# Radial products on halves of the array's rows, with the bias added by bf16 products of ones

## The reference

```python
R = relu(abs_distances[:, None] @ w1 + b1) @ w2 + b2      # (E, 384), HIDDEN = 64
Y = spherical_harmonics(rel_vec)
Fj = features[src]
...
acc = acc + _NORM[i] * jnp.einsum('euv,ef,evi,ofi->euo', Rb[..., k], Yf, Fb, C)
...
out = out.at[dst].add(msg)
x = _layernorm(x + out)
```

## Time and profile before

| | |
|---|---|
| time, median of 3 runs | 1985.52 us (1982.97 to 1986.45) |
| span of the profiled execution | 1707.1 us |
| median less span | 278.4 us |
| busy in the span: PE, DVE, POOL, ACT | 1315.9, 1193.5, 1068.9, 858.9 us |
| mean granted TensorE clock | 0.846 of full speed |
| layer 1 | 1139 to 1556 us |

### The profile page before, as it was taken

How to read it: one execution, slowest core, us unless ns; L and a number is a source line. 1 busy time by engine, 2 the same in 40 slices (tenths; PEclk the granted TensorE clock), 3 DMA queues, 4 the chain that set the end, 5 groups by cost and what they waited for, 6 DMA issues and landing times.

```text
span 1707.1 us, 25367 instructions
## 1 busy us (share of the span) xinstructions
PE 1315.9 (77%) x6200; PEld 957.6 (56%) x6200; DVE 1193.5 (70%) x3648; ACT 858.9 (50%) x2256; POOL 1068.9 (63%) x1168
## 2 busy tenths in 40 slices
PE   5699993686513777665778999958999999996673
PEld 1388881242212555554655666635777777775563
DVE  9699995677512443676667999964777777774776
ACT  0167770011101222666775777735666666664884
POOL 7777778777777777774111444448877887830444
PEclk8599996577555999888888999977999999997655
DMA  1000000123224988665555666531222222213785
GB/s 41 13 14 13 14 14 20 47 72 79 67 68 127 257 250 246 171 174 145 132 138 140 179 184 189 163 95 32 58 58 57 58 64 67 59 42 78 196 216 157
DMA packets 298498, 178.98 MB, mean 105 GB/s; under 512 B 28715, under 2 KB 290032, under 8 KB 298352
## 3 DMA queue, kind: packets, MB, share of 16 engines
q1 hardware_dynamic: 219712, 116.54, 26.0%
q0 software_dynamic: 29008, 36.18, 8.3%
q10 hardware_dynamic: 49632, 24.65, 5.0%
HBM read 111.18 MB, written 66.07 MB: 104 GB/s over the span
## 4 chain that ended last, share of the span: by engine, by line
PE 42%; POOL 28%; issue 16%; DVE 8%; DMA 2%; DVEq 2%; SPq 1%; ACT 1%; POOLq 0%; ACTq 0%
PE bank L1025 12%; POOL gat L511 12%; POOL lined L518 11%; PE bank L994 7%; PE bank L1018 7%; DVE res L1308 5%; PE bank L945 3%; POOL out L591 3%; PE bank L947 3%; PE bank L1034 3%; PE bank L1003 3%; PE bank L987 3%; DMA placed<-pay,pos_i 1%; DVEq L1308 1%; DVEq L1302 1%
## 5 line engine op out<-in xcount | busy, mean ns | idle before, releaser
L566 POOL DMA_INDIRECT gat<-x_d,src_i x196 | 253.2, 1292 | 59.0 <-issue 53.1
L511 POOL DMA_INDIRECT gat<-in_x,key_i x196 | 211.1, 1077 | 64.8 <-issue 62.4
L1308 DVE TENSOR_TENSOR res<-res,bank 128x128 f32 x588 | 168.4, 286 | 108.5 <-issue 24.4
L528 POOL DMA_INDIRECT placed<-pay,pos_i x196 | 191.9, 979 | 68.1 <-issue 65.6
L518 POOL DMA_INDIRECT lined<-in_x,other_i x196 | 195.8, 999 | 59.7 <-issue 59.7
L1025 PE MATMUL bank<-prod,ident 128*128 128x280 f32 x896 | 217.0, 400 | 0.0
L1025 PEld LDWEIGHTS bank<-prod,ident 128*128 128x128 f32 x896 | 171.0, 191 | 46.5 <-issue 0.6
L956 PE MATMUL bank<-woh,pw 128*128 128x128 f32 x784 | 135.4, 335 | 69.3 <-DVE woh L1287 33.4
L956 PEld LDWEIGHTS bank<-woh,pw 128*128 128x128 f32 x784 | 120.3, 238 | 85.5 <-DVE woh L1287 44.5
L56 ACT ACTIVATE xt<-bank 128x128 f32<-128x128 f32 x98 | 26.6, 271 | 269.6 <-PE bank L897 261.2
L1018 PE MATMUL bank<-rw,ht 65*128 65x384 f32 x392 | 141.3, 514 | 23.3 <-ACT ht L738 13.8
(11 more groups left out here) (204 smaller groups left out, 2840.5 us busy)
## 6 DMA issues: line engine op xcount, KB each, us to landing
pw<-placed SPq DMA_DIRECT2D x588, 68.0 KB, 2.1
pw<-placed SPq DMA_DIRECT2D x98, 272.0 KB
xin<-in_x_t SPq DMA_DIRECT2D x53, 256.0 KB, 3.2
placed<-pay SPq DMA_DIRECT2D x49, 272.0 KB, 2.4
x_d<-res POOLq DMA_DIRECT2D x49, 256.0 KB, 3.8
placed<-pay SPq DMA_DIRECT2D x28, 448.0 KB, 3.2
out<-out ACTq DMA_DIRECT2D x49, 256.0 KB, 2.7
xin<-in_x_t ACTq DMA_DIRECT2D x45, 256.0 KB, 3.6
```

The source lines that it names most:

```text
L511: pool.indirect_dma_start(gat[:, t, :], None, x, bass.IndirectOffsetOnAxis(ap=key_i[:, 0, t:t + 1], axis=0)).then_inc(s_gat, 16)
L528: pool.indirect_dma_start(placed[1].rearrange("t p r -> (t p) r"), bass.IndirectOffsetOnAxis(ap=pos_i[:, 1, t:t + 1], axis=0), pay[i % 4][ ...
L566: pool.indirect_dma_start(gat1[g % 3][:, k, :], None, x1_d, bass.IndirectOffsetOnAxis(ap=src_i[:, t:t + 1], axis=0)).then_inc(c_gat[g % 3] ...
L1308: add.up(dve.tensor_tensor(into, into, quarter(bank + k // G, k % G), ALU.add))
```

## The change

The products of R are split by the array's rows. `arow` and `ht` get 128 partitions: the tiles of a group with even numbers (0, 2, 4, 6) stand in partitions 0 to 63, those with odd numbers (1, 3, 5) in partitions 64 to 127, each 128 edges wide, so `ht[h]` is 128 partitions by 512 columns. `rw`, `rwc_sb` and their raw forms are held twice, once in each half. The row of ones is gone, so an f32 product has 64 rows. The bias is added by a bf16 product of its own in front of it, into the same bank: `unit`, ones of 64 rows by 128 columns, is held, and `rb3`, 64 rows by 384, is streamed, whose rows 0, 1 and 2 are the bias in three bf16 pieces that add up to it, the others zero. PE goes through a group in three pairs and a single tile: both waits for the banks and both products of ones stand in front of the two f32 products.

SP issues two DMAs for `arow` instead of one, and reads every second row of `ew_d` in each. The weights' DMAs move behind a wait for `s_rec` (line 1183's signal), in front of the first store of the placed rows, because `rw_raw` now shares memory with earlier arrays; there are 4 of them instead of 1, and one more for `rwc_sb`. DVE's `radial_weights` places and scales the bias too and splits it. A memset of `arow`'s spare corner takes the place of the memset of ones.

```diff
@@ load_weights, SP
-                sp.dma_start(arow[h][:, :].rearrange("p (t q) -> p t q", t=U),
-                             ew_d[U * g:U * g + U, :].partition_broadcast(HID)).then_inc(c_arow[h], 16)
+                for o in range(2):
+                    n = (U + 1 - o) // 2
+                    sp.dma_start(arow[h][HID * o:HID * o + HID, 0:P * n].rearrange("p (t q) -> p t q", t=n),
+                                 ew_d[U * g + o:U * g + U:2, :].partition_broadcast(HID)).then_inc(c_arow[h], 16)
@@ in front of SP's stores of the placed rows
+            sp.wait_ge(s_rec, 1)
+            for h in range(2):
+                sp.dma_start(rw_raw[HID * h:HID * h + HID, :], rwb[0:HID, :]).then_inc(s_rwld, 16)
+                sp.dma_start(rb_raw[HID * h:HID * h + HID, :], rwb[HID:HID + 1, :].partition_broadcast(HID)).then_inc(s_rwld, 16)
@@ hidden_3, ACT
-                act.wait_ge(c_arow[h], 16 * (g // 2 + 1))
+                act.wait_ge(c_arow[h], 32 * (g // 2 + 1))
-                act.activation(ht[h][0:HID, :], arow[h][:, :], ACT.Relu, bias=rwc_sb[:, 1:2], scale=rwc_sb[:, 0:1]).then_inc(c_ht, 1)
+                act.activation(ht[h][:, :], arow[h][:, :], ACT.Relu, bias=rwc_sb[:, 1:2], scale=rwc_sb[:, 0:1]).then_inc(c_ht, 1)
@@ radial, PE
-                for k in range(U):
-                    n = U * g + k
-                    wait(pe, c_rsb, n - 2)
-                    pe.matmul(psum[n % 3][:, 0:RC], ht[g % 2][:, P * k:P * k + P], rw[:, :, :].rearrange("p a b -> p (a b)"),
-                              start=True, stop=True).then_inc(c_r, 1)
+                for k in range(0, U, 2):
+                    pair = [(U * g + k + o, HID * o) for o in range(min(2, U - k))]
+                    for n, r in pair:
+                        wait(pe, c_rsb, n - 2)
+                        pe.matmul(psum[n % 3][:, 0:RC], unit[r:r + HID, :], rb3[r:r + HID, :, :].rearrange("p a b -> p (a b)"),
+                                  start=True, stop=False)
+                    for n, r in pair:
+                        pe.matmul(psum[n % 3][:, 0:RC], ht[g % 2][r:r + HID, P * (k // 2):P * (k // 2) + P],
+                                  rw[r:r + HID, :, :].rearrange("p a b -> p (a b)"), start=False, stop=True).then_inc(c_r, 1)
@@ radial_weights, DVE (combine(to, raw) is the 7 instructions of before)
+                dve.memset(unit[:, :], 1.0)
+                chain.up(combine(rw, rw_raw))
+                done(chain)
+                chain.up(combine(rb, rb_raw))
+                chain.up(dve.tensor_scalar(half[:, :], pcol[:, :], float(HID), -float(HID), ALU.is_ge, ALU.mult))
+                done(chain)
+                chain.up(dve.tensor_tensor(half[:, :], half[:, :], pcol[:, :], ALU.add))
+                done(chain)
+                for n in range(3):
+                    chain.up(dve.tensor_scalar(piece[:, n:n + 1], half[:, :], float(n), None, ALU.is_equal))
+                for n in range(3):
+                    chain.up(dve.tensor_copy(rb_h[:, :, :], rb[:, :, :]))
+                    done(chain)
+                    if n == 0:
+                        ins = dve.tensor_scalar(rb3[:, :, :], rb_h[:, :, :], piece[:, 0:1], None, ALU.mult)
+                    else:
+                        ins = dve.scalar_tensor_tensor(out=rb3[:, :, :], in0=rb_h[:, :, :], scalar=piece[:, n:n + 1], in1=rb3[:, :, :],
+                                                       op0=ALU.mult, op1=ALU.add)
+                    if n == 2:
+                        ins.then_inc(s_rw, 1)
+                    else:
+                        chain.up(ins)
+                        chain.up(dve.tensor_tensor(rb[:, :, :], rb[:, :, :], rb_h[:, :, :], ALU.subtract))
+                        done(chain)
@@ DVE, ahead of layer 1
-                dve.memset(ht[h][HID:HID + 1, :], 1.0).then_inc(s_ones, 1)
+                dve.memset(arow[h][HID:P, P * (U // 2):P * UP], 0.0).then_inc(s_spare, 1)
```

More of the change, by code:

```diff
@@ L30 @@
 NU = NT // U
-BU = U * P
+UP = (U + 1) // 2
 ROW = P + 8
@@ L125, in gnn_kernel @@
         start_i = sb_e("start_i", [1, NW], I32)
[L126 to L131, removed]
+        vectors, sb_v = scope()
+        relsq = sb_v("relsq", [P, NT, 3])
+        rsum = sb_v("rsum", [P, NT])
+        rnorm = sb_v("rnorm", [P, NT])
+        rinv = sb_v("rinv", [P, NT])
+        iota_i = sb_v("iota_i", [P, NW], I32)
+        vectors.close()
+        rw_raw = sb_e("rw_raw", [P, RC])
+        rw_t = sb_e("rw_t", [P, 8, 8])
+        rb_raw = sb_e("rb_raw", [P, RC])
+        rb = sb_e("rb", [P, 16, 24])
+        rb_h = sb_e("rb_h", [P, 16, 24], BF16)
+        half = sb_e("half", [P, 1])
+        piece = sb_e("piece", [P, 3])
         early.close()
@@ L147, in gnn_kernel @@
         bias = sb("bias", [P, 4])
-        rwc_sb = sb("rwc_sb", [HID, 2])
-        rw = sb("rw", [HID + 1, 16, 24])
+        rwc_sb = sb("rwc_sb", [P, 2])
+        rw = sb("rw", [P, 16, 24])
+        rb3 = sb("rb3", [P, 16, 24], BF16)
+        unit = sb("unit", [P, P], BF16)
         kr = sb("kr", [P, NT])
@@ L193, in gnn_kernel @@
         other_f = sb1("other_f", [P, NT])
-        iota_i = sb1("iota_i", [P, NW], I32)
         pcol_i = sb1("pcol_i", [P, 1], I32)
@@ L229, in gnn_kernel @@
         gat1 = ring(sb3, "gat1", 3, [P, U, D])
-        arow = ring(sb3, "arow", 2, [HID, BU])
-        ht = ring(sb3, "ht", 2, [HID + 1, BU])
+        arow = ring(sb3, "arow", 2, [P, UP * P])
+        ht = ring(sb3, "ht", 2, [P, UP * P])
         rsb = sb3("rsb", [P, U, 16, 24])
@@ L286, in gnn_kernel @@
         m_sum, m_hx, m_sq, m_ssq, m_root, m_x1 = sem("m_sum"), sem("m_hx"), sem("m_sq"), sem("m_ssq"), sem("m_root"), sem("m_x1")
-        m_st, s_rw, s_ones = sem("m_st"), sem("s_rw"), sem("s_ones")
+        m_st, s_rw, s_rwld, s_spare = sem("m_st"), sem("s_rw"), sem("s_rwld"), sem("s_spare")
         c_gat, c_arow, c_pst, c_away, c_oh = ring(sem, "c_gat", 3), ring(sem, "c_arow", 2), ring(sem, "c_pst", 2), sem("c_away"), sem("c_oh")
@@ L423, in _ @@
             sp.dma_start(bias[:, :], b0).then_inc(s_wld, 16)
-            sp.dma_start(rwc_sb[:, :], rwc).then_inc(s_wld, 16)
-            sp.dma_start(rw_raw[:, :], rwb).then_inc(s_wld, 16)
+            for h in range(2):
+                sp.dma_start(rwc_sb[HID * h:HID * h + HID, :], rwc).then_inc(s_wld, 16)
             sp.wait_ge(s_zero, 1)
@@ L778, in _ @@
             act.wait_ge(m_x1, NB)
-            act.wait_ge(s_ones, 2)
+            act.wait_ge(s_spare, 2)
             hidden_3(0)
@@ L1009, in _ @@
             pe.wait_ge(s_rw, 1)
-            pe.wait_ge(s_ones, 2)
             pe.wait_ge(m_x1, NB)
@@ L1248, in _, with combine @@
             ins.then_inc(s_order, 1)
[L1250 to L1258, removed]
+            def combine(to, raw):
+                b = [raw[:, 64 * n:64 * n + 64].rearrange("p (u v) -> p v u", v=8) for n in range(3)]
+                b11 = raw[:, 192:384].rearrange("p (u v k) -> p v u k", v=8, k=3)
+                dve.tensor_scalar(to[:, 0:8, 0:8], b[0], C_00, None, ALU.mult)
+                dve.tensor_scalar(to[:, 8:16, 0:8], b[1], C_00, None, ALU.mult)
+                dve.tensor_scalar(to[:, 0:8, 8:16], b[2], C_10, None, ALU.mult)
+                dve.tensor_scalar(to[:, 8:16, 8:16], b11[:, :, :, 2], C_11_2, None, ALU.mult)
+                dve.tensor_scalar(to[:, 8:16, 16:24], b11[:, :, :, 1], C_11_1, None, ALU.mult)
@@ L1259, in radial_weights @@
                 chain.up(dve.tensor_scalar(rw_t[:, :, :], b11[:, :, :, 2], -C_11_2 / 3.0, None, ALU.mult))
                 done(chain)
-                dve.scalar_tensor_tensor(out=rw[:, 0:8, 16:24], in0=b11[:, :, :, 0], scalar=C_11_0, in1=rw_t[:, :, :],
-                                         op0=ALU.mult, op1=ALU.add).then_inc(s_rw, 1)
+                return dve.scalar_tensor_tensor(out=to[:, 0:8, 16:24], in0=b11[:, :, :, 0], scalar=C_11_0, in1=rw_t[:, :, :],
+                                                op0=ALU.mult, op1=ALU.add)
@@ new lines, in radial_weights @@
+            def radial_weights():
+                dve.wait_ge(s_rwld, 64)
+                dve.memset(unit[:, :], 1.0)
[15 more added lines that the diff above has]
+                        ins = dve.scalar_tensor_tensor(out=rb3[:, :, :], in0=rb_h[:, :, :], scalar=piece[:, n:n + 1], in1=rb3[:, :, :],
+                                                       op0=ALU.mult, op1=ALU.add)
+                    if n == 2:
[4 more added lines that the diff above has]
+                        done(chain)
```

## The result

| | before | after |
|---|---|---|
| median of 4 runs each | 1985.99 us (1982.97 to 1987.79) | 1997.76 us (1990.95 to 1998.77) |
| ratio, 95% interval | | 1.0056 (1.0033 to 1.0079) |
| one group in the steady stretch of layer 1 | 13.63 us | 14.07 us |

The change costs 11.8 us by the medians, 0.56% by the ratio. The forecast was +28 us: the sign and the stage were right, the size was 2.4 times too large.

The account below looks back on a forecast made before the run. PE was taken to bound layer 1 at 13.63 us a group. Bank loop 0.88 plus array changes 0.16 gave 1.04 us for 27 groups, +28 us: 2014 us, range 1987 to 2036.

Parts of the forecast that it names:

- PE bounds layer 1, and each 0.1 us a group counts: Layer 1: PE alone fills the 13.63 us group, so 0.1 us there is 0.1 us of kernel, for about 27 groups.
- The trips of the banks decide, so that overlap cannot pay: Radial products: waits for three banks make a loop of 1.77 us per pair, against 1.29 before; +0.88 us a group.
- the likeliest case: The bank loop as worked out: +1.04 us a group, +28 us; own range +12 to +33 us; chance 0.50.
- ones to f32 0.28: Radial products: 0.28 us from a bf16 product of ones to the f32 product behind it, at four places a group.
- Records of one tile keep b0 ahead of a1: PE order a0, b0, a1, b1 (first and second f32 records of tiles 0 and 1): a1 at best runs beside b0.
- one slot in four: Radial products: the most that overlap of the array's halves would save in a pair's four f32 records.
- Two changes of mode, 0.16 a group, at most 0.33: PE going between whole and half array twice a group: from nothing to 0.33 us, half taken, 0.16.
- drains: At each change between whole and half array, PE waits for the last product's end: 0.163 us each, the upper bound.
- Ones as added work: Seven added bf16 products of ones in the radial products: laid end to end, 1.62 us a group.
- ACT, SP, DVE's weights at nothing: Relu and copies, added DMAs and new wait, and about 6.3 us of DVE weights: each 0, covered by idle time or distance.
- No overlap: Rival: the halves' radial products run one after the other; +1.63 us a group, +44 us, 2030 us; chance 0.28.
- The free halves: Rival: halves overlap freely, loop under 1.5 us, radial products 4.06 us; -0.46 us a group, -12 us, 1973 us; chance 0.13.

Follow-up runs that it names:

- one half: Changed kernel with both tiles of a pair on rows 0 to 63, so nothing can overlap; 2028.46 us, ratio 1.0210 to the kernel before, 15.07 us a group.
- pairs with four banks: Changed kernel with a fourth PSUM bank for R, so a tile waits for the copy of n - 4; ratios to the kernel before 0.9923 and, again, 0.9932.
- merges in between: Changed kernel with a fourth bank, merges moved between the second and third pair of radial products; 1983.20 us, ratio 0.9939 to the kernel before.
- alternating rows: Kernel before with f32 products of 64 rows instead of 65 for tiles 1, 3 and 5, without their bias; 2021.72 us, ratio 1.0143.
- 64 rows: Kernel before with all f32 products of R on 64 rows instead of 65 and no bias; 1716.40 us, ratio 1.0099, 14.01 us a group.

## Why the prediction was right in sign and wrong in size

The account of one group, each term from a run:

| term | us | from |
|---|---|---|
| seven products of ones at 0.165 | +1.15 | one half |
| changes of mode (0.10 on entry, ones in front; 0.19 on exit) | +0.29 | one half: 0.43 - 0.33; 7.74 - 7.55 |
| overlap of the halves | -2.11 | pairs with four banks 12.96 against one half 15.07 |
| trips of the banks | +1.11 | the change 14.07 against pairs with four banks 12.96 |
| sum | +0.44 | 14.07 - 13.63 |

The last two terms both still hold the one trip that four banks leave, so each is a lower bound of its size; their sum is exact.

Over the kernel: the first sums start at 1446.2 and the last group's end with a start at 1827.6 in the change, 1447.2 and 1819.1 in the kernel before.

```profile
L1044 PE MATMUL bank<-prod,ident x896: 398/400/504, 1446.2 to 1827.6; 128*128 128x280 f32 x180
```

```profile
L1025 PE MATMUL bank<-prod,ident x896: 397/399/674, 1447.2 to 1819.1; 128*128 128x280 f32 x180
```

That is 381.4 - 371.9 = +9.5 us for the 27 distances between groups: 24 at +0.44, one at +0.71, the last at +0.10, and the first 1.83 shorter than before (12.93 us against 14.76). That first difference is no merit of the change: its group ran at a granted clock of 1.00, that of the kernel before at 0.84. The measured 11.8 us (interval 6.6 to 15.7) agrees.

*PE bounds layer 1, and each 0.1 us a group counts.* Right.

*The trips of the banks decide, so that overlap cannot pay.* Right as a mechanism for this order of the list, shown by the fourth bank; with each tile's ones directly in front of its f32 product, three banks were enough for a gain. The size was wrong, and this is the term that failed: the likeliest case priced a trip at 1.77 us and the radial products at +0.88 a group. The trip takes 1.49, and the products, taken out of the change of mode, 4.67 instead of 5.40. Pick-up, copy, return and the two f32 records were right (0.20, 0.49, 0.05, 0.65), and so was the 0.10 for a load behind the wait, though it is the f32 product's and not that of the ones: together 1.49. Wrong was "ones to f32 0.28". It was taken four times: twice in the trips (0.56), at the first tile (0.11 too much: a0 starts 1567.04 - 1566.87 = 0.17 after the ones) and at the seventh (about 0.12 too much). In the trips it is zero, because the ones that are waited for are those of the other half: tile 2's f32 product, whose own ones had started at 1567.68, is held up by that wait and starts at 1568.49, together with them. And one half shows that even on the same rows the transition costs nothing. In the earlier trace rows the f32 product stood behind two waits of its own; I took the gap for a price of the data types, and it is likely that of the waits, which no run tested in that place. The four places together are 0.79 us; the products were forecast 5.40 - 4.67 = 0.73 us too long, so all else came out 0.06 too short. The changes of mode, 0.13 too low, went the other way: 1.04 - 0.73 + 0.13 = 0.44. That the lower end of the likeliest case, +12 us or 0.43 a group, meets the result is luck: it left 0.167 in at each of the four places and put the changes of mode at nothing.

*Records of one tile keep b0 ahead of a1.* Wrong, without effect on the sum: a1 starts with a0, two records of 0.48 us within 0.48 us from 1567.04 on. The loop of the banks hid the mistake here, but the same assumption made a gain of more than "one slot in four" look impossible, and with four banks a pair that waits for nothing takes 0.16 + 0.65 = 0.81 us (in the run with merges in between), where one half takes 0.33 + 1.29 = 1.62.

*Two changes of mode, 0.16 a group, at most 0.33.* Wrong the other way. 0.29 in the change, 0.38 with f32 products at both ends, 0.195 each in the run with alternating rows: one change between f32 products costs more than my upper bound for it, the 0.163 by which one record overlaps the next. That this overlap is what a change costs (the "drains" of the forecast's range) was my estimate, and no run shows it; the runs show 0.10 and 0.19 us in its place. The held operand's load is not hidden either: the record behind the change is 0.59 us long instead of 0.49. That load also starts later: in the run with 64 rows 0.21 us after the start of the last product ahead of it (1303.89 against 1303.68); with 65 rows, in the kernel before, the two start together (both at 1292.34). This term is 0.29 of the 0.44 us that the change lost, and a row count of 64 instead of 65, with nothing else, costs 0.38 us.

*Ones as added work.* In the likeliest case rightly hidden within the trips; without them a group is only 0.12 us shorter.

*ACT, SP, DVE's weights at nothing.* Right for the time. DVE's weights took 17 us in the profile, 686.0 to 703.4, not 7.5, with waits of about 2 us in them that I had not counted. The payloads on either side start at 685.3 and 703.3 us, where the kernel before has 685.3 and 687.1. But the next stage's gathers start for the last time at 1052.6 us, against 1052.7 before: the delay was made up.

*The rivals.* No overlap (+1.63 a group) is refuted, and one half shows what it would have cost: +1.44, of which 1.15 are the ones, too high in the forecast by the same 0.28, and 0.29 the changes of mode, which it had left out. The free halves (-0.46) deserved more than their chance of 0.13 for the mechanism, though not for the time: their condition, the f32 product starts as soon as the bank is back, holds, with a trip of 1.49 us against the 1.5 named. Their sum had the two trips in it and came out 0.90 us too low: it left out the first and seventh ones (0.33), the changes of mode (0.29) and, for most of the rest, the loads of f32 products behind a wait (about 0.10 each).

## What to carry to other kernels

In this kernel the work that overlaps needed buffers for all that was in flight: a pair has two banks being filled while two are emptied, so three banks turned a gain of 0.8% into a loss of 0.6%, and one idle bank or another order of the list was the whole difference. Put a wait directly in front of the work that needs it, not in front of its neighbour's too (13.40 us a group here, against 14.07). Count how often TensorE goes between products of 64 rows and larger ones (0.19 us each time here between f32 products, 0.10 into a bf16 one), and read a price between two instructions only where no wait stands between them.

## What the runs showed of the hardware that was not expected

Going from products of 65 rows to products of 64 or back costs 0.195 us (5.69 - 4.52 for six changes), even though both kinds start at row 0.

One program takes 1701.5 us on one chip and 1987.4 or 1992.4 on two others. Most of the difference lies near the start. The table by stretches, first the profile ahead of the prediction, then the kernel before on a slower chip:

```profile
50.00:285.00 235.00, 197.74 (x1057) 161.91 (x1058) 206.69 (x949) 126.59 (x353) 179.65 (x172) 0.88 0.09 13
```

```profile
70.00:285.00 215.00, 40.12 (x116) 25.26 (x115) 27.73 (x124) 12.96 (x40) 143.59 (x150) 0.52 0.08 12
```

POOL goes at nearly one pace in both (172 and 150 instructions); PE, DVE and ACT start an eighth to a ninth of the instructions in the second. The list of waits (who waited, for whom, us in total, times, longest) says "issue" for much of it, that is, the profile shows nothing that the engine waited for:

```profile
PEld bank L868 <- issue: 108.1, 10, 33.3
...
DVE sel L1202 <- issue: 51.5, 13, 10.6
```

POOL's first 196 gathers start between 3.8 and 261.1 us there, and by 285 us the other engines are back at a usual pace. Its next 196 (line 518) start between 448.9 and 724.6 us, where the profile ahead of the prediction has 277.5 to 531.7. So 171 of the 272 us by which the first radial product is later (1416.5 against 1144.3) arise ahead of these gathers, 21 in them, and 60 in the 196 behind them (line 528: 734.0 to 1052.7, against 533.0 to 791.7). Why this comes on some chips and not on others stays open; no run was made for it. The difference is some 24 times as large as the change studied here.
